# A four-layer graph network: the opening of layer 3 is moved into the last graphs of layer 2

## What is computed

```
h1, h2, h3 = inp @ W1, inp @ W2, inp @ W3
e = leaky_relu(h1 @ h2.T, 0.2)
e = where(adj > 0, e, -1e12)
x = x + relu(softmax(e) @ h3)
```

## Time and profile before

| | |
|---|---|
| median of 3 runs | 2105.55 us (2104.94 to 2108.16) |
| the profiled execution | 2097.68 us, its span 2095.8 us |
| TensorE (PE) busy | 79% of the span |
| VectorE (DVE) busy | 76% |
| ScalarE (ACT) busy | 64% |
| GpSimd (POOL) busy | 6% |
| mean granted TensorE clock | 0.905 of full |

### The profile page before, as it was taken

One profiled execution on the slowest core, in us unless ns is written; L12 is line 12 of the kernel. 1 busy time (PEld: TensorE's weight loads), 2 busy tenths in 40 slices (PEclk: granted clock), 3 DMA queues, 4 the chain that ended last, 5 costly groups with the idle time before them and its releaser, 6 DMA issues. The chain is left out here.

```text
span 2095.8 us, 36839 instructions
## 1 busy us (share of the span) xinstructions
PE 1662.8 (79%) x13620; PEld 1056.3 (50%) x13620; DVE 1600.5 (76%) x2710; ACT 1339.4 (64%) x1751; POOL 124.7 (6%) x130
## 2 busy tenths in 40 slices
PE   2888877888778657799998976777877657999997
PEld 1333333433334336677776765556655553455544
DVE  3676867878778855788888999898898856766674
ACT  2665645656556448676677798898888834455453
POOL 0000100101100010000000000000000000000000
PEclk7988989899999859899999988889998879999999
DMA  7545263352533231111111111122211211000000
GB/s 208 131 101 122 64 145 86 93 134 69 134 93 102 69 114 42 41 42 44 48 41 52 41 68 66 62 63 72 70 64 62 71 56 40 11 11 20 10 11 20
DMA packets 74923, 146.51 MB, mean 70 GB/s; under 512 B 11937, under 2 KB 34722, under 8 KB 74754
## 3 DMA queue, kind: packets, MB, share of 16 engines
q1 hardware_dynamic: 74754, 144.23, 24.4%
HBM read 101.85 MB, written 8.78 MB: 53 GB/s over the span
## 5 line engine op out<-in xcount | busy, mean ns | idle before, releaser
L1068 ACT ACTIVATE g<-s_all,steep_d 128x1024 fp8e4<-128x1024 f32 x608 | 642.4, 1136 | 39.6 <-DMA s_all<-s_rows 18.4
L1003 PE MATMUL acc<-parts,g 128*128 128x102 bf16 (+1 forms) x6144 | 414.1, 228 | 29.3 <-DVE sums L1159 21.7
L1003 PEld LDWEIGHTS acc<-parts,g 128*128 128x128 fp8e4 x6144 | 398.2, 99 | 62.3 <-issue 45.6
L985 PE MATMUL post<-parts,edge 128*128 128x396 bf16 (+1 forms) x1024 | 232.4, 383 | 86.4 <-DVE base L1167 86.4
L561 ACT ACTIVATE e<-s_ps 128x1024 f32<-128x1024 f32 x256 | 248.6, 1023 | 24.8 <-PE s_ps L420 18.3
L1152 DVE TENSOR_TENSOR g<-g,edge 128x1024 int32<-128x1024 int32 x192 | 228.0, 1219 | 34.6 <-ACT g L1068 34.6
L706 DVE SCALAR_TENSOR_TENSOR e<-e,bound 128x1024 f32<-128x1024 f32 x160 | 188.8, 1214 | 34.6 <-ACT e L561 33.5
L416 PE MATMUL s_ps<-qs,ks 128*128 128x512 f32 x512 | 200.6, 503 | 9.9 <-issue 8.0
L432 PE MATMUL sum_ps<-e,pick 128*32 128x256 f32 x2048 | 144.5, 402 | 71.7 <-DVE e L703 42.5
L985 PEld LDWEIGHTS post<-parts,edge 128*128 128x128 fp8e4 x1024 | 101.8, 102 | 193.4 <-issue 107.9
L567 ACT ACTIVATE chunk<-ctx_ps 128x512 f32<-128x512 f32 x128 | 76.4, 597 | 178.6 <-PE ctx_ps L441 178.6
(11 more groups left out here) (158 smaller groups left out, 2117.1 us busy)
## 6 DMA issues: line engine op xcount, KB each, us to landing
s_all<-s_rows SPq DMA_DIRECT2D x96, 512.0 KB, 3.6
inv_all<-inv_rows SPq DMA_DIRECT2D x256, 128.0 KB, 2.9
qs<-split SPq DMA_DIRECT2D x128, 128.0 KB, 3.1
ks<-split SPq DMA_DIRECT2D x128, 128.0 KB, 2.4
x<-in_x SPq DMA_DIRECT2D x8, 512.0 KB, 6.8
inv_rows<-inv SPq DMA_DIRECT2D x32, 128.0 KB, 1.7
adj_in<-in_adj SPq DMA_DIRECT2D x8, 512.0 KB, 4.3
out_x<-x SPq DMA_DIRECT2D x8, 512.0 KB, 3.2
```

The source lines that it names most:

```text
L985: ins = pe.matmul(self.post[:, it % 2, 0:H * 3 * W1].rearrange("p (h k c) -> p h k c", h=H, k=3), self.c.edge[:, jt, it * P:(it + 1) * P], ...
L1003: ins = pe.matmul(self.acc[:, bank, o:o + self.NS], self.g[:, h % RING, jt, it * P:(it + 1) * P], self.upper[par][:, jt, h, :, :].rearrang ...
L1068: act.activation(self.g[:, h % RING, jt, :], self.s_all[:, h % 2, :], ACT.Relu, bias=self.steep_d[par][:, jt, h:h + 1], scale=STEEP, satur ...
```

## The change

The opening of layer 3 becomes a class of its own. Its tiles (bias, first ht, first q) lie in `parts[0]`, now called the arena and allocated for the whole kernel; its three weights and the folded one have buffers that outlive the block. Its steps are called from layer 2's last two graphs (B - 2 is graph 6, B - 1 is graph 7):

| engine | graph 6 | graph 7 |
|---|---|---|
| SP | weights behind head 0; adjacency tiles 0 to 3 behind heads 1, 3, 5, 7 | tiles 4 to 7 behind heads 4 to 7, each with a wait on a bias |
| VectorE | | statistics in head 0; bias tiles 0 to 3 in heads 1 to 4, 4 and 5 in head 6, 6 and 7 in head 7 |
| GpSimd | | rstd |
| ScalarE | | folded weights and h in head 3, copy to ht in head 6, copy to q in head 7 |
| TensorE | | folded weights in head 0, turn in head 2, query in head 4 |

The adjacency goes through four buffers of its own, and transfers wait on the bias four tiles before. `layer3` begins with the scores. In the arm for wide weights the same steps run in a block by themselves. The diff, cut:

```diff
@@ class Shared @@
-        self.parts = [sb(f"parts{i}_", [P, T * 8 * 3 * 2 * 17]) for i in range(2)]
+        self.parts = [c.arena, sb("parts1_", [P, T * 8 * 3 * 2 * 17])]
@@ new @@
+class Opening:
+    def __init__(self, c, w):
+        a = c.arena
+        self.bias = a[:, 0:T * HALF].bitcast(BF16).rearrange("p (t n) -> p t n", t=T)
+        self.ht, self.q = a[:, T * HALF:T * HALF + N], a[:, T * HALF + N:T * HALF + 2 * N]
...
+    def sp_adj(self, sp, adj_in, tiles):
+        for t in tiles:
+            if t >= 4:
+                sp.wait_ge(self.adj_used, t - 3)
+            sp.dma_start(adj_in[:, t % 4, :], self.w["adj"][t * P:(t + 1) * P, :]).then_inc(
+                self.adj_loaded[max(t // 2 - 1, 0)], 16)
+    def pe_w12(self, pe, aux):
+        pe.wait_ge(self.loaded, 48)
+        pe.matmul(aux[:, 0:F], self.w1_t, self.w2_t, start=True, stop=True).then_inc(self.w12_projected, 1)
+    def pe_turn(self, pe, aux):
+        pe.wait_ge(self.w12_ready, 1)
+        self.norm(aux).pe_turn(pe, 0, 0)
+    def pe_q(self, pe, aux):
+        nm = self.norm(aux)
+        pe.wait_ge(nm.h_t_ready, nm.upto(0))
+        project_rows(pe, aux, self.w12[:, :], self.ht).then_inc(self.q_projected, 1)
...
+    def dve_bias(self, dve, adj_in, tiles):
+        for t in tiles:
+            dve.wait_ge(self.adj_loaded[max(t // 2 - 1, 0)], 64 if t < 4 else 32)
+            dve.tensor_scalar(self.bias[:, t, :], adj_in[:, t % 4, :], 0, NEG, ALU.is_le, ALU.mult).then_inc(self.adj_used, 1)
@@ additive_layers: SP @@
                     a.sp_head(sp, b, par, h)
+                    if a is two and isinstance(b, int) and b == B - 2:
+                        if h == 0:
+                            third.sp_weights(sp)
+                        elif h % 2 == 1:
+                            third.sp_adj(sp, adj_in3, (h // 2,))
+                    elif a is two and isinstance(b, int) and b == B - 1 and h >= 4:
+                        third.sp_adj(sp, adj_in3, (h,))
@@ TensorE, behind the head's matmuls @@
+                    if a is two and isinstance(b, int) and b == B - 1:
+                        if h == 0:
+                            third.pe_w12(pe, aux)
+                        elif h == 2:
+                            third.pe_turn(pe, aux)
+                        elif h == 4:
+                            third.pe_q(pe, aux)
@@ ScalarE, behind the head's g @@
+                        if h == 3:
+                            third.act_w12(act, aux)
+                            third.norm(aux).act_h(act, 0, 0)
+                        elif h == 6:
+                            third.act_h_t(act, aux)
+                        elif h == 7:
+                            third.act_q(act, aux)
@@ VectorE, behind the next head's g and the sums @@
                     pieces(dve, 2 * h + 2, a, b, par, soon, later)
+                        if h == 0:
+                            third.dve_stats(dve, aux)
+                        elif h < 5:
+                            third.dve_bias(dve, adj_in3, (h - 1,))
+                        elif h > 5:
+                            third.dve_bias(dve, adj_in3, (2 * h - 8, 2 * h - 7))
                     if h == 2:
                         a.dve_base(dve, b, (2, 3))
                     if before and h == 1:
@@ layer3: SP, GpSimd, TensorE, ScalarE and VectorE each lose their part @@
-            for dst, name in ((w1_t, "w1_t"), (w2_t, "w2_t"), (w3, "w3")):
-                sp.dma_start(dst[:, :], w[name]).then_inc(loaded, 16)
-            for t in range(T):
-                if t >= 2:
-                    sp.wait_ge(adj_used, t - 1)
-                sp.dma_start(adj_in[:, t % 2, :], adj[t * P:(t + 1) * P, :]).then_inc(adj_loaded[t % 2], 16)
...
-            def prepare(n, par):
-                stats(n, par)
-                for t in range(T):
-                    dve.wait_ge(adj_loaded[t % 2], 16 * (t // 2 + 1))
-                    dve.tensor_scalar(bias[:, t, :], adj_in[:, t % 2, :], 0, NEG, ALU.is_le,
-                                      ALU.mult).then_inc(adj_used, 1)
-                dve.wait_ge(adj_used, T)
```

More of the change, by code:

```diff
@@ new lines, in open_apart, with _ @@
+def open_apart(c, opening):
+    with ExitStack() as ctx:
+        adj_in = c.sb("adj_in_w3", [P, 4, N], I32, ctx)
+        aux = c.ps("aux_w3", [P, N], ctx)
+        block = ctx.enter_context(c.nc.Block())
+        @block.sync
+        def _(sp):
+            opening.sp_weights(sp)
+            opening.sp_adj(sp, adj_in, range(T))
+        @block.gpsimd
+        def _(pool):
+            opening.norm(aux).pool_rstd(pool, 0)
+        @block.tensor
+        def _(pe):
+            opening.pe_w12(pe, aux)
+            opening.pe_turn(pe, aux)
+            opening.pe_q(pe, aux)
+        @block.scalar
+        def _(act):
+            opening.act_w12(act, aux)
+            opening.norm(aux).act_h(act, 0, 0)
+            opening.act_h_t(act, aux)
+            opening.act_q(act, aux)
+        @block.vector
+        def _(dve):
+            opening.dve_stats(dve, aux)
+            opening.dve_bias(dve, adj_in, range(T))
@@ L1233, in walk_both, with additive_layers @@
     tail()
-def additive_layers(c, w1, w2):
+def additive_layers(c, w1, w2, third):
     nc = c.nc
@@ L1249, in additive_layers @@
         both = (one, two)
+        adj_in3 = c.sb("adj_in3", [P, 4, N], I32, ctx)
+        aux = two.aux
         block = ctx.enter_context(nc.Block())
@@ L1293, in stage @@
                     at[0].pool_top(pool, at[1])
+                elif b == B - 1:
+                    third.norm(aux).pool_rstd(pool, 0)
             walk_both(pool, both, prepare, stage, lambda: None)
@@ L1663, in _, with layer3 @@
             graphs(dve, graph, tile)
-def layer3(c, x_out, adj, w):
+def layer3(c, x_out, opening):
     nc = c.nc
@@ L1671, in layer3 @@
         sb = lambda name, shape, dt=F32: c.sb(name, shape, dt, ctx)
[L1672 to L1677, removed]
+        bias, w3, w12 = opening.bias, opening.w3, opening.w12
+        q = [opening.q, sb("q3_1", [P, N])[:, :]]
+        ht = [opening.ht, sb("ht3_1", [P, N])[:, :]]
         z = sb("z3", [P, 2, N])
@@ L1691, in layer3 @@
         nm = Norm(c, 3, aux)
-        loaded, adj_loaded, adj_used = sem("weights"), [sem("adj_a"), sem("adj_b")], sem("adj_used")
-        w12_projected, w12_ready = sem("w12_projected"), sem("w12_ready")
-        q_projected, q_ready = sem("q_projected"), sem("q_ready")
+        q_projected, q_ready = opening.q_projected, opening.q_ready
         s_ready, biased, minus_ready, shift_ready, leaky = (
@@ L1727, in stage @@
                     nm.pool_rstd(pool, b + 1)
-            walk(pool, lambda n, par: nm.pool_rstd(pool, n), stage)
+            walk(pool, lambda n, par: None, stage)
         @block.tensor
         def _(pe):
-            pe.wait_ge(loaded, 48)
-            pe.matmul(o_ps[:, 0:F], w1_t[:, :], w2_t[:, :], start=True, stop=True).then_inc(w12_projected, 1)
             def turn(n, par):
@@ L1787, in project @@
                 for i in range(Q):
-                    ins = pe.matmul(r_ps[:, i, :], o_sb[:, i * P:(i + 1) * P], w3[:, :], start=True, stop=True)
+                    ins = pe.matmul(r_ps[:, i, :], o_sb[:, i * P:(i + 1) * P], w3, start=True, stop=True)
                 ins.then_inc(r_projected, 1)
@@ L1817, in tail @@
                 project(2 * B - 1)
-            walk(pe, prepare, stage, tail)
+            walk(pe, lambda n, par: None, stage, tail)
         @block.scalar
         def _(act):
-            act.wait_ge(w12_projected, 1)
-            act.activation(w12[:, :], o_ps[:, 0:F], ACT.Copy).then_inc(w12_ready, 1)
             def h(n, par):
@@ L1895, in tail @@
                 scaled(2 * B - 1, 1)
-            walk(act, prepare, stage, tail)
+            walk(act, lambda n, par: None, stage, tail)
         @block.vector
@@ L1968, in tail @@
                 update(2 * B - 1, B - 1, 1)
-            walk(dve, prepare, stage, tail)
+            walk(dve, lambda n, par: None, stage, tail)
 def build(nc, a, out, layers=(0, 1, 2, 3)):
@@ L1978, in build @@
         c.edge = c.sb("edge", [P, T, N], F8)
+        c.arena = c.sb("arena", [P, T * 8 * 3 * 2 * 17], F32)
+        opening = Opening(c, a)
         w1, w2 = ({"wv": a[f"w_{n}"], "w_out_t": a["w_out_t"], "adj": a["adj"], "adj_t": a["adj_t"]} for n in HEADS)
@@ L1981, in build @@
         with nc.If(wide == 0):
-            sems = additive_layers(c, w1, w2)
+            sems = additive_layers(c, w1, w2, opening)
         with nc.Else():
@@ L1985, in build @@
             additive_layer_wide(c, 2, w2, sems[1])
+            open_apart(c, opening)
         if 3 in layers:
-            layer3(c, out, a["adj"], a)
+            layer3(c, out, opening)
             return
```

33 lines of the change are left out of this document (25 added, 8 removed).

## The result

Over 7 runs of each on one chip the changed kernel took 2085.99 us in the median (2078.21 to 2088.77), the kernel before 2099.5 (2094.33 to 2108.16). The ratio is 0.9925 with a 95% interval of 0.9899 to 0.9951. Ten runs more on another occasion gave 2087.82 against 2100.64, ratio 0.9953 (0.9929 to 0.9977). The ratio is an estimate over the runs as a whole, not the quotient of the two medians. By the two ratios the kernel is 0.5 to 0.8% faster, 10 to 16 us; the medians differ by 13.5 and 12.8 us. The profiled execution took 2088.77 us, its span was 2087.0.

What follows compares the result with a forecast made beforehand. Adjacency transfers with bias, and beside them the chain to the query, were taken to bound layer 3's opening. Border -18.6, last graph +4.8, load +0.4 gave -13.4 us, from median 2105.55 to 2092; range 2086 to 2101.

Steps and rivals of the forecast that it cites:

- The border: From layer 2's last update of x to layer 3's first mask: 27.0 us shrink to 8.4, so 18.6 go.
- both must leave: At layer 3's opening, bias and the chain to the query must both go; moving bias alone leaves first scores ending at 1737.0.
- because two buffers allow only two tiles in flight: At layer 3's opening, the reason given for VectorE's 14.6 us idle before the bias instructions, waiting for adjacency transfers.
- The combine moves by 1.95: Layer 2's last graph: statistics 2.7 less 1.5 of waits plus 0.7 first bias delay VectorE's long combine 1.95 us, one for one.
- TensorE's 2.6 in the dense part: Layer 2's last graph: turn of h (0.87 us) and query rows (1.72) add 2.6 us to TensorE's nearly gapless last part.
- VectorE's 0.3 behind TensorE: End of layer 2's last graph: with the last four bias tiles, VectorE reaches the last sums 0.3 us after TensorE's head 7.
- s_all, 0.4: Graph 6's head 7: adjacency tile 3 delays this load by 1.5 us, ScalarE's wait hides most, leaving 0.4 us.
- even split: Graph 6's head 7: transfers sharing engines evenly would double the load's 3.7 us, costing 2.5 instead of 0.4, result 2094.3.
- its wait ahead of head 6's g: Layer 2's last graph: ScalarE's 5.75 us wait for TensorE absorbs 3.5 us of added work and shrinks to about 4.
- Not slower by the clock: Slower rival, layer 2's last graph: TensorE's longer pause keeps its clock low, 25 us more, 2117 us; chance 0.04.
- taking the same 13.4 off the median gives 2092: Whole kernel: the 13.4 us gain, derived from the profiled execution, is subtracted from the runs' median of 2105.55 us.
- the better case: Rival: layer 2's waits absorb all but TensorE's 2.6 us and first scores run fast; 17.4 us gained, 2088; chance 0.14.

## Why the prediction was right or wrong

**The change** was forecast as 13.4 us. In the two traces of each kernel, last graph and border take 98.3 and 97.7 us before, 83.8 and 83.4 after: 14.4 us in the mean. The medians differ by 13.5 and 12.8; that one of them meets the 13.4 is luck. By its own steps:

- *The border*, 27.0 to 8.4: it is 8.7 and 8.5. The branch kept its 4 us, and the scores took 3.78, not 3.43. Right, and both halves were needed, as "both must leave" said; the bias alone was to leave about 24 us and left 25.8. Only "because two buffers allow only two tiles in flight" holds in part: four buffers shortened the stretch of the transfers by 3.4 us, no more.
- *The combine moves by 1.95*: by 1.53, and one for one into TensorE's base matmuls.
- *TensorE's 2.6 in the dense part*: from the start of the base matmuls to head 7's end 2.24 more (36.65 against 34.41), since the low clock left these matmuls earlier (5.05 us instead of 5.47). With the two steps moved away, TensorE's head 7 ended 2.66 us sooner (60.44 and 57.78), so their price was right.
- *VectorE's 0.3 behind TensorE*: its last sums end 3.8 later, head 7 3.8. Level, as nearly as the trace tells. Together 3.8 where I had 4.8, and just under the "4 to 6 us later" for the last update. Taking only 0.3 for the last tiles was right because TensorE's work hid them: with that work moved away, VectorE's last sums still end 2.5 later than before the change, of which the combine's move explains 1.5.
- *s_all, 0.4*: ScalarE's wait before graph 6's head 7 is 3.20 us, 2.84 in the trace of before. Over all twelve traces it is 2.93 to 3.22 us in the seven with a tile right behind this load, and 2.84 to 2.97 in the five without. So the tile costs the load 0 to 0.4 us, far from the 3.7 of an even split. The Trainium skill (DMA: Bandwidth & Descriptors, Issuing engines are not separate DMA queues) says only that the transfers interleave on the same 16 engines; the even split was the prediction's own reading of it, and no trace bears that reading out. That nothing of it reached the end is a reading of graph 6's length (62.0 and 61.3 before, 61.0 and 62.0 after, ends of updates of graphs 4 and 5), not an experiment by itself.
- *ScalarE*: its wait ahead of head 6's g went from 5.75 to 4.74 us (forecast: about 4), and TensorE's query rows did not wait for the copy of h.
- *Not slower by the clock*: TensorE's pause was 10.05 us, not longer than before, and the clock came back during the base matmuls.

**The number** was not right. 2085.99 lies just under the range's lower end of 2086. The step that failed is the last of the sum, "taking the same 13.4 off the median gives 2092", with the range's "spread of the runs of 3 us". That median stood on three runs within 3.2 us of each other. Later sets of 7 (with those three), 27, 18 and 17 runs gave medians of 2099.5, 2100.64, 2099.36 and 2100.05, and single runs from 2090.09 to 2110.53. So the base was 5 to 6 us high and the spread some 20 us, where I had allowed 3: 2099.5 - 13.4 would have been 2086.1. The range does not follow its own terms either: the better case of 2088 less 3 is 2085, not 2086. The measured median fell 0.01 us outside; to be inside or outside by so little is chance; the 6 us between 2092 and the measured median are the base. The profiled execution of 2097.68, which I noted as "0.4% under the median", was a sign of this, and I took the ratio of the two for a constant. Where the spread comes from is told by the traces only in part: it lies mostly in layers 0 to 2 (from layer 3's first mask to the end all twelve traces have 355.3 to 357.7 us), and in layer 2's loop it goes with TensorE's granted clock; why the clock is granted low more often in one execution is open.

## What to carry to other kernels

When two chains of nearly equal length fill a gap, moving one of them gains little (here nothing that stood clear of noise); move both, and count each path's end. Put moved work not where an engine is busy on average least, but into the waits of the chain that ends last: here the same work cost 3.8 us up to the last sums when it all lay in the busy heads, 1.1 with TensorE's two steps and four bias tiles in the gaps behind them, and nothing with the rest in waits too. A forecast of a change is worth no more than the level that it is taken from: ask how far single runs stray, before a range gets its width.

## What was not expected of the hardware

A TensorE that idles in a chain makes the next steps slower too: with the gaps filled by work that nobody needs, the last projection took 2.05 us instead of 3.78, and the last graph got shorter. It did not carry over 5.06 us of standing still: the first scores took 3.78 us with and without. And a loop of identical graphs took 262.7 to 272.0 us in different executions, with a granted clock of 0.87 in one graph and 0.83 in the same graph of another.
